# A graph message-passing layer on one core: edge factor applied in the sort, one one-hot for both sums, VectorE on pairs of units

## What is computed

```python
xn = layernorm(h) * ln_w + ln_b
w_phys = (silu(rbf @ w1 + b1) @ w2 + b2) * cutoff[:, None]      # one filter row of 256 for each edge
msg_phys = xn[col] * w_phys
q_e, k_e, v_e = Q[row], K[col], V[col]                          # 8 heads of 32
scores = sum(q_e * k_e, axis=-1) / sqrt(32) * cutoff[:, None]
attn = softmax(scores, axis=1)                                  # over the 8 heads of one edge
combined = msg_phys + gate * (attn[..., None] * v_e)
aggr = segment_sum(combined, row)
out = x + h + aggr @ wo + bo
```

## Time and profile before

| | |
|---|---|
| median of 3 runs | 5557.56 us (5555.09 to 5559.14) |
| profiled execution, its own time | 5559.19 us |
| its span, first to last instruction | 5557.3 us |
| busy: PE, PEld, DVE, ACT, POOL | 93%, 70%, 81%, 59%, 72% |
| mean granted TensorE clock | 0.972 of full |

### The profile page before, as it was taken

How to read it: one execution, slowest core, us unless ns; L and a number is a source line. 1 busy time by engine, 2 the same in 40 slices (tenths; PEclk the granted TensorE clock), 3 DMA queues, 4 the chain that set the end, 5 groups by cost and what they waited for, 6 DMA issues and landing times. The chain is left out here.

```text
span 5557.3 us, 119878 instructions
## 1 busy us (share of the span) xinstructions
PE 5156.6 (93%) x24352; PEld 3906.9 (70%) x24353; DVE 4493.7 (81%) x11381; ACT 3260.9 (59%) x11609; POOL 4001.3 (72%) x3475
## 2 busy tenths in 40 slices
PE   3879999999999999995899999999999999999999
PEld 3556666666666666674677777777777777777777
DVE  9789887666655555323899999999999999999995
ACT  4223333333333333332788888888888888888884
POOL 1567777777777777775577777777777777777770
PEclk9889999999999999997899999999999999999999
DMA  6234444444444443445999999999999999999965
GB/s 200 89 105 133 144 165 158 142 150 167 158 145 148 168 155 134 152 156 181 314 320 326 325 326 326 325 321 326 325 326 325 326 325 327 324 326 327 326 198 185
DMA packets 584358, 1305.93 MB, mean 235 GB/s; under 512 B 81230, under 2 KB 384118, under 8 KB 582945
## 3 DMA queue, kind: packets, MB, share of 16 engines
q0 software_dynamic: 221536, 881.08, 44.7%
q1 hardware_dynamic: 311780, 345.48, 20.5%
q10 hardware_dynamic: 50850, 77.03, 3.9%
HBM read 1024.15 MB, written 324.38 MB: 243 GB/s over the span
## 5 line engine op out<-in xcount | busy, mean ns | idle before, releaser
L1002 POOL DMA_INDIRECT ukvx<-kvx_table,udst x1760 | 2174.7, 1236 | 668.3 <-issue 480.9
L338 POOL DMA_INDIRECT records<-rows,slot_i x1660 | 1750.9, 1055 | 666.6 <-issue 498.2
L691 PE MATMUL w_ps<-w2s,hid 128*128 128x256 f32 x6656 | 1555.7, 388 | 47.4 <-DVE rows L605 47.3
L691 PEld LDWEIGHTS w_ps<-w2s,hid 128*128 128x128 f32 x6656 | 1251.4, 193 | 371.9 <-issue 156.9
L805 ACT ACTIVATE hid<-hid_ps,b1t 128x512 f32<-128x512 f32 x832 | 525.5, 682 | 1518.5 <-PE hid_ps L680 1504.1
L605 DVE TENSOR_TENSOR rows<-w_ps,b2b 128x512 f32<-128x512 f32 x832 | 570.9, 686 | 749.0 <-PE w_ps L691 748.9
L1118 PE MATMUL ag_ps<-ukvx,uonehot_cut 128*128 128x256 f32 x3520 | 989.3, 404 | 5.3
L1103 PE MATMUL uq_ps<-aggr,uonehotT 128*128 x3520 | 986.4, 404 | 0.0
L1122 PE MATMUL ag_ps<-ukvx,uonehot 128*128 128x256 f32 x3520 | 941.2, 392 | 41.1 <-ACT uonehot L1036 41.1
L1122 PEld LDWEIGHTS ag_ps<-ukvx,uonehot 128*128 128x128 f32 x3520 | 689.0, 196 | 139.7 <-issue 42.2
L1118 PEld LDWEIGHTS ag_ps<-ukvx,uonehot_cut 128*128 128x128 f32 x3520 | 604.8, 192 | 153.9 <-issue 6.3
(11 more groups left out here) (171 smaller groups left out, 5025.0 us busy)
## 6 DMA issues: line engine op xcount, KB each, us to landing
urec<-records SPq DMA_DIRECT2D x880, 260.0 KB
rbf_in<-in_edge_attr SPq DMA_DIRECT2D x207, 256.0 KB, 2.9
kvx_table<-kvx ACTq DMA_DIRECT2D x10, 3456.0 KB, 14.7
ukvx<-kvx_table,udst POOLq DMA_INDIRECT x1760
records<-rows,slot_i POOLq DMA_INDIRECT x1661, 2.6
records<-kvx SPq DMA_DIRECT2D x1, 13000.0 KB
fbase<-x_plus_h SPq DMA_DIRECT2D x14, 896.0 KB, 7.2
out<-fout SPq DMA_DIRECT2D x13, 896.0 KB, 4.9
```

The source lines that it names most:

```text
L338: pool.indirect_dma_start(recs, bass.IndirectOffsetOnAxis(ap=slot_i[:, q, t:t + 1], axis=0), rows[:, q, t, :], None).then_inc(scattered[q] ...
L691: m = pe.matmul(w_ps[j % 2][:, h, :], hid[:, k % 2, c, h, j * P:(j + 1) * P], w2s[:, c, :], start=(h == 0 and c == 0), stop=(c == 1), skip ...
L1002: pool.indirect_dma_start(kvx[:, k, j, :], None, table, bass.IndirectOffsetOnAxis(ap=dst_i[:, k, j:j + 1], axis=0), bounds_check=NPAD - 1, ...
```

## The change

- In the sort, ScalarE multiplies each filter row by its edge factor in place (`scale`, four tiles at a time; the first half of a group at the end of its own iteration, the second in the next), and the scatter waits for the two halves (`scaled`) instead of `w_out` and `placed`.
- In the edge stage the one-hot times factor and the one-hot times reciprocal are gone. One float32 copy of the one-hot (`widen`) serves both sums; VectorE multiplies the exponentials by the reciprocal (`normalise`) ahead of `attend`.
- `physical`, `score`, `weigh`, `maximum`, `invert`, `normalise`, `attend` and `select` each take two units with one instruction, in every second unit; `select` is one `tensor_tensor` over four halves instead of two `tensor_scalar` a unit. `exponent` handles a pair too. `query_key` stays one instruction a unit.
- `half_bucket` has bytes instead of int32. TensorE loads 32 numbers a turn, ScalarE 16, both from an offset that is a multiple of 16.

The core of the diff:

```diff
-        half_bucket = sb("half_bucket", [1, HALVES + 2 * DEPTH], I32)
+        half_bucket = sb("half_bucket", [1, HALVES + 2 * SEEN], U8)
 
         prep(nc, sem, x, src, dst, rbf, weight, w1, b1, w2, b2, ln_w, ln_b, wq, bq, wk, bk, wv, bv, wo, bo,
...
                 q = k % RING
-                pool.wait_ge(s["w_out"], g * 4 + 4)
-                pool.wait_ge(s["placed"], g + 1)
-
-                pool.sem_inc(s["placed_waited"], 1)
                 tail = isinstance(g, int) and g == LASTG
                 for t in range(LASTC if tail else GC):
+                    if t % 4 == 0:
+                        pool.wait_ge(s["scaled"], g * 2 + t // 4 + 1)
+                        pool.sem_inc(s["scaled_seen"], 1)
                     pool.indirect_dma_start(recs, bass.IndirectOffsetOnAxis(ap=slot_i[:, q, t:t + 1], axis=0),
                                             rows[:, q, t, :], None).then_inc(scattered[q], 16)
                 if tail:
+                    pool.wait_ge(s["scaled"], g * 2 + 2)
...
+            def scale(g, k, half):
+
+                q = k % RING
+                act.wait_ge(s["w_out"], g * 4 + 2 * half + 2)
+                if half == 0:
+                    act.wait_ge(s["placed"], g + 1)
+                    act.sem_inc(s["placed_seen"], 1)
+                for t in range(4 * half, 4 * half + 4):
+                    m = act.activation(rows[:, q, t, 0:H], rows[:, q, t, 0:H], ACT.Copy, scale=rows[:, q, t, R_CUT:R_CUT + 1])
...
+                        scale(g - 1, (k - 1) % BODY, 1)
                     if more:
                         silu(g + 1, k + 1, 1)
                     if more2:
                         evacuate(g + 2, k + 2)
+                    scale(g, k, 0)
                     if t is not None:
                         act.wait_ge(s["xnt_ps"], (i - 1) * NB + t + 1)
                         act.activation(xnT[:, t].rearrange("p k e -> p (k e)"), tq_ps[:, 0:H], ACT.Copy).then_inc(s["xnt_sb"], 1)
...
             act.wait_ge(s["q_stored"], 16 * BATCHES)
...
-                    sp.wait_ge(s["cut_ready"], u - (DEPTH - 1))
+                    sp.wait_ge(s["onehot_ready"], u - (DEPTH - 1))
...
+            def widen(u, k, i, first):
                 act.wait_ge(s["onehot_ready"], u + 1)
                 if not first:
                     act.wait_ge(s["ag_done"], u - (DEPTH - 1))
-                for j in range(2):
-                    m = act.activation(ohc[:, k, j, :], ohb[:, k, j, :], ACT.Copy, scale=rec[:, k, j, R_CUT:R_CUT + 1])
-                m.then_inc(s["cut_ready"], 1)
-
-            def share(u, k, i, first):
-                act.wait_ge(s["recip_done"], u + 1)
-                for j in range(2):
-                    m = act.activation(oh[:, k, j, :], ohb[:, k, j, :], ACT.Copy, scale=rc[:, k % 2, j:j + 1])
-                m.then_inc(s["share_ready"], 1)
+                act.activation(oh[:, k], ohb[:, k], ACT.Copy).then_inc(s["widened"], 1)
...
+                q = k // 2 % 2
                 act.wait_ge(s["max_done"], u + 1)
-                if not (first and k < 2):
-                    act.wait_ge(s["av_done"], u - 1)
-                for j in range(2):
-                    m = act.activation(ex[:, q, j, :], sc[:, q, j, :], ACT.Exp, bias=mx[:, q, j:j + 1], accum_out=sm[:, q, j:j + 1])
-                m.then_inc(s["exp_ready"], 1)
+                if not (first and k < 4):
+                    act.wait_ge(s["av_done"], u - 3)
+                for r in range(4):
+                    m = act.activation(ex[:, q, r, :], sc[:, q, r, :], ACT.Exp, bias=mx[:, q, r:r + 1], accum_out=sm[:, q, r:r + 1])
+                m.then_inc(s["exp_ready"], 2)
...
+                        half_bucket[0:1, 0:2 * DEPTH] if first else half_bucket[0:1, bass.ds(u * 2, 2 * DEPTH)],
...
-                exponent(u, k, i, first)
+                if k % 2:
+                    exponent(u, k, i, first)
                 if not (first and k < LAG):
-                    keep(u - LAG, bucket_of[k])
+                    keep(u - LAG, bucket_of[2 * k + 1])
...
+            _, rest = nc.values_load_multi_w_load_instructions(half_bucket[0:1, HALVES:HALVES + 2 * DEPTH], engines=[mybir.EngineType.Activation], min_val=0, max_val=BUCKETS - 1,
...
-                    pe.matmul(to[j], ohc[:, k, j, :], kvx[:, k, j, 2 * H:3 * H], start=False, stop=False, skip_group_check=True)
+                    pe.matmul(to[j], oh[:, k, j, :], kvx[:, k, j, 2 * H:3 * H], start=False, stop=False, skip_group_check=True)
                 pe.wait_ge(s["av_done"], u + 1)
-                pe.wait_ge(s["share_ready"], u + 1)
...
-                dve.wait_ge(rec_in[k], i * 16 + 16)
+                for n in range(2):
+                    dve.wait_ge(rec_in[k + n], i * 16 + 16)
                 if not first:
-                    dve.wait_ge(s["cut_ready"], u - (DEPTH - 1))
-                    dve.wait_ge(s["share_ready"], u - (DEPTH - 1))
-                    dve.wait_ge(s["turned"], u - (DEPTH - 1))
-                for j in range(2):
-                    m = dve.tensor_scalar(ohb[:, k, j, :], iota_bf[:], rec[:, k, j, R_LOC:R_LOC + 1], None, ALU.is_equal)
-                m.then_inc(s["onehot_ready"], 1)
+                    dve.wait_ge(s["widened"], u - (DEPTH - 2))
+                    dve.wait_ge(s["turned"], u - (DEPTH - 2))
+                dve.tensor_tensor(pair(ohb, k), iota_bf[:].unsqueeze(1).to_broadcast([P, 4, P]),
+                                  pair(rec, k)[:, :, R_LOC:R_LOC + 1].to_broadcast([P, 4, P]), ALU.is_equal).then_inc(s["onehot_ready"], 2)
...
+                dve.wait_ge(kvx_in[k + 1], i * 32 + 32)
+                both = pair(kvx, k)[:, :, 2 * H:3 * H]
+                dve.tensor_tensor(both, pair(rec, k)[:, :, 0:H], both, ALU.mult).then_inc(s["phys_done"], 2)
...
             def score(u, k, i, first):
...
-                    dve.wait_ge(s["exp_ready"], u - 1)
...
+                dve.tensor_reduce(sc[:, q], pair(kvx, k - 1)[:, :, 0:H].rearrange("p r (h d) -> p r h d", h=NH), AX_X, ALU.add).then_inc(s["scored"], 2)
...
-                dve.tensor_reduce(mx[:, q], sc[:, q], AX_X, ALU.max, negate=True).then_inc(s["max_done"], 1)
+                dve.tensor_reduce(mx[:, q], sc[:, q], AX_X, ALU.max, negate=True).then_inc(s["max_done"], 2)
...
+                dve.reciprocal(sm[:, q], sm[:, q]).then_inc(s["recip_done"], 2)
+
+            def normalise(u, k, i, first):
+                q = k // 2 % 2
+                dve.wait_ge(s["recip_done"], u + 1)
+                dve.tensor_tensor(ex[:, q], ex[:, q], sm[:, q].unsqueeze(2).to_broadcast([P, 4, NH]), ALU.mult).then_inc(s["shared"], 2)
...
+                dve.wait_ge(s["shared"], u + 1)
+                values = pair(kvx, k - 1)[:, :, H:2 * H].rearrange("p r (h d) -> p r h d", h=NH)
+                dve.tensor_tensor(values, values, ex[:, q].unsqueeze(3).to_broadcast([P, 4, NH, HD]), ALU.mult).then_inc(s["av_done"], 2)
...
                 query_key(u, k, i, first)
-                physical(u, k, i, first)
-                ahead(select, SELECT_AHEAD, u, k, i, first, last)
-                score(u, k, i, first)
-                behind(invert, 1, u, k, i, first)
-                weigh(u, k, i, first)
-                maximum(u, k, i, first)
-                behind(attend, 1, u, k, i, first)
+                if k % 2 == 0:
+                    physical(u, k, i, first)
+                    behind(invert, 1, u, k, i, first)
+                    behind(normalise, 1, u, k, i, first)
+                    behind(attend, 1, u, k, i, first)
+                else:
+                    score(u, k, i, first)
+                    weigh(u, k, i, first)
+                    maximum(u, k, i, first)
+                    ahead(select, SELECT_AHEAD - 1, u, k, i, first, last)
```

71 lines of the change are left out of this document (31 added, 40 removed).

## The result

The changed kernel takes 6550.82 us (median of 4 runs, 6548.81 to 6557.02), the kernel before, run beside it, 5557.38: a ratio of 1.179, 95% interval 1.1769 to 1.181. 993 us more, where the prediction had 48 less.

The account below looks back on a forecast made before the run. VectorE bounds the edge stage, TensorE nearly equal. 5559.2 - 51 (edge stage) + 4 (sort +3, last scatters -2, filling and draining +3) = 5512, less 1.6 for the median: 5510 us; 8 in 10 for 5468 to 5562.

Parts of the forecast that it names:

- Register loads: Once-a-turn loads in the edge stage, priced by 16-byte pieces: TensorE's 32 bytes 1.07 us, ScalarE's 16 bytes 0.85.
- its alternative: TensorE's register load priced by number, 64 ns each, so that it goes up by 0.32 us.
- the rival: ScalarE's load alone could double to 3.4 us with 16 numbers: 33 us, giving 5543; within a rival of chance 0.22.
- VectorE's pair: VectorE's edge-stage steps for two units: 6.19 us against 6.26 before, 3.10 a unit, dependent starts 0.04 us after their cause.
- The slack of 1.9 us: Queries done 1.9 us before VectorE wants them, covering the once-a-turn stall of 1.3; TensorE catches up 0.46 us a pair.
- TensorE becomes the bound: Rival: load by number, or stall and clock unchanged; 3.13 to 3.17 us a unit, 5518 to 5552 us; chance 0.22.
- Late records: Rival: edge-stage record loads landing after more than 6.9 us; 0.2 over gives 88 us, 5570 to 5620; chance 0.13.
- Gathers: GpSimd's two gathers a unit, 1.52 and 1.00 us, the long one containing the selects; with the new select 1.0 for both.
- the sort: ScalarE's scale passes, 0.516 us each, cost the sort 3 us; earlier scatters of the last group give -2.
- the DMA engines as no bound: Edge-stage DMA, bytes unchanged: a unit could go down to 2.71 us, so no bound at 3.12.
- passes over four rows: VectorE's passes over a pair occupy 1.13 to 1.14 us; rival that they cost two passes: 5545 to 5565, chance 0.10.
- the select at 0.61: VectorE's new select, one instruction a pair, forecast at 0.60 us against 0.66 for a pair's selects before.

Follow-up runs that it names:

- e1: The changed kernel with int32 bucket numbers again instead of bytes; 5851.92 us, 1.0522 of the kernel before.
- e5: e1 with each pair pass raising its semaphore by one instead of two; 5900.68 us, 1.0612 of the kernel before.
- e9: e5 with the select moved into the even unit, behind physical and the reciprocal; 5653.7 us, 1.0172 of the kernel before.
- e14: e5 with TensorE's register load split into 20 numbers at a turn's first unit and 12 at the fifth; 5760.97 us, 1.0373 of the kernel before.
- e7: e6 with the edge factor copied out by ScalarE, so record loads no longer wait for the pair's weights; 5572.99 us, 1.0036 of the kernel before.
- e8: The kernel before with the change's aligned loads of 32 and 16 numbers, as int32, and nothing else of it; 5539.7 us, 0.9966 of the kernel before.
- e12: e8 with TensorE's register load split into 20 and 12 numbers; 5521.17 us, 0.9933 of the kernel before.
- e13: e7 with TensorE's register load split into 20 and 12 numbers; 5410.08 us, 0.9736 of the kernel before.
- e6: e5 with the select in the even unit and attend in the odd unit; 5590.16 us, 1.0059 of the kernel before.

## Why the prediction was wrong

**Register loads: the step that failed.** The prediction read four durations as pieces of 16 bytes, 256 and 290 ns each, and so had 32 bytes at 1.07 us. Measured: 7.55. Four int32 values fill such a piece, so the same rows read "64 ns a value", which the text had as its alternative. But that alternative took the price of an int32 for a byte, +0.32 us. Both readings were fitted on int32 alone; a value of another width was outside the rows, and no row bounded it from above. The dear price stood in the earlier trace rows already, ScalarE's 1724 ns for eight, and the fit by pieces explained it away. The term that was mis-sized is 1.07 us against 7.55, 110 times; against int32 loads of the same count the bytes cost 699 us, the low clock behind them included. The Trainium skill (Runtime: NRT & Kernel Launch, Instruction fetch mechanics) has some 200 ns a register, of registers that are loaded from HBM. For bytes the runs agree within a fifth, 235 ns on TensorE and 3396/16 = 212 on ScalarE; for int32 in a row they do not, 64. The prediction quoted it with 6.4 us for this load, close to the 7.55, and then priced the rival with ScalarE's load alone, because TensorE's 87 ns seemed to refute the rule. It refuted it for int32 in a row only. By that page, 6.4 - 2.35 = 4.1 us in 110 turns would have been an estimate of 450 us more, and that belonged in the range. Without the bytes the forecast would have failed as well: e1's 5852 us lie 290 above the range, by the next two steps.

**VectorE's pair: right in its passes, wrong in its gaps.** Forecast 6.19, measured 6.68. Of the 0.49 us between them, 0.30 are five dependent starts that came 0.10 instead of 0.04 us after their cause, 0.12 the step from maximum to select (0.23 where 0.11 stood), and only 0.07 the passes themselves. With increments of one (e5) the pair is 6.3, so most of the difference is the waits that stand as instructions of their own. The prediction took the gap from the old code, where each rise was one, and did not see that the diff changes the increments. It had (6.26 - 6.19) x 440 = 31 us won by the pairs; (6.7 - 6.26) x 440 = 194 us were lost, in e1 as in the changed kernel. Even the 6.3 of e5 is not below the 6.26 of before: in the order of the change, pairs save VectorE nothing.

**The slack of 1.9 us did not exist.** The prediction let TensorE catch up 0.46 us a pair and so cover the pause. But the turn of a pair's first unit needs the select, now the last step of the pair: TensorE waits for it (159.9 us, 173 times), and what it would gain in pace it can't store ahead of the load. e9 and e14 show both sides of this, 1.4 and 1.3 us a turn of the 3.6 left over in e5. The stall makes up the rest of e1's 290 us, about 100.

**"TensorE becomes the bound": right in kind, too small.** The rival had 3.13 to 3.17 us a unit by a pause of 1.3 and 0.8 us of clock. e7, with VectorE at 2.94, ran at 3.22. The pause is 1.3 by PE's own row; by the row of PEld it was 174.4/102 = 1.7 before, and 197.0/100 = 2.0 in e7. e8 shows that already the kernel before paid for over half of it. That VectorE and TensorE were nearly equal bounds, 25.0 and 25.1 us a turn, fits the runs with int32 loads of the same count: beside e8, the change with its quickest pairs is 33 us slower (e7), the split load alone 19 us faster (e12), and both together are 130 us faster (e13). Why e7 is slower than e8, with less work on VectorE and the same load, stays open.

**Late records: the mechanism is there, its price depends on the rest.** In the changed kernel the median landing is 5.5 us, inside the 6.9 allowed, though ScalarE waits for records 121 times from 2750 to 5300 us, 139.1 us in all; what that costs there no run shows. In e6 and e9 the wait is longer, and freeing the buffer early is worth 17 us in the one and 76 in the other, close to the rival's 88.

**Gathers: the wrong culprit.** The prediction blamed the selects for 1.52 against 1.00. In the changed kernel, from 3998.87 on, with attend from 3998.87 to 4000.10 and the select from 4002.64 to 4003.33:

```profile
3998.44 1.01 POOL L1018 DMA_INDIRECT ukvx<-kvx_table,udst  x1 [0.30 <-issue]
3999.75 1.22 POOL L1018 DMA_INDIRECT ukvx<-kvx_table,udst  x1 [0.30 <-issue]
4001.28 1.01 POOL L1018 DMA_INDIRECT ukvx<-kvx_table,udst  x1 [0.30 <-issue]
4002.59 1.01 POOL L1018 DMA_INDIRECT ukvx<-kvx_table,udst  x1 [0.30 <-issue]
```

Only the one that starts while attend is running is long: 0.35 us of attend were left, and 0.35 + 0.88 = 1.23. Of the 521 gathers from 2700 us on that start while attend or physical alone is running, 519 last what is left of the pass plus 879 ns, within 15 ns; the 320 that start under the score, which has one input, last 1.00 to 1.02 us. In the earlier trace rows the long gather starts at 3992.52, 0.04 after physical, and 0.64 + 0.88 = 1.52: physical, not the select inside it. Nor is the new select harmless, as the prediction had it. In the changed kernel hardly a gather starts under it (4), but in e5 317 do, and 316 of them are long by the same sum, as this one:

```profile
4007.91 0.69 DVE L1181 TENSOR_TENSOR uonehot_bf<-uiota_bf,urec 128x512 bf16<-128x512 bf16 x1
4008.11 1.37 POOL L1021 DMA_INDIRECT ukvx<-kvx_table,udst  x1 [0.30 <-issue]
```

The Trainium skill (SBUF — State Buffer, Who interferes with whom) says that a VectorE instruction with two inputs in SBUF contends with a GpSimd instruction that reads SBUF. These rows agree, if the gather counts as one (its `udst` lies in SBUF), and the prediction had used only what the passage says of `tensor_scalar`. No run shows a time that hangs on it; in the changed kernel GpSimd was not the bound.

**Right:** the sort (+1 us forecast, 1.0005 measured; the scale passes take 505 ns against 516 forecast), the DMA engines as no bound down to 3.04 us a unit (333 GB/s), passes over four rows at 1.13 us, and the select at 0.61.

## What to carry over

Where one engine's instruction stream pauses once a turn, ask what is queued on it just then: a step that was moved to the end of its pair emptied the queue, and a pause that had been covered in part cost its full length and the low clock behind it. Two bounds that are equal must be relieved together; each alone gives little. A price read from rows of one width, count or increment holds for that one: when the diff changes any of them, the range has to reach as far as the dearest rule at hand.

## What was not expected of the hardware

- A register load of bytes costs 234 to 235 ns a value on TensorE and 212 on ScalarE, of int32 in a row 64 on both. ScalarE's every second one of 16 int32 costs 215 each, as bytes do. 32, 20, 16 and 12 int32 took TensorE 2134, 1372, 1112 and 848 ns; 27 and 7 took 2348 and 1066, about 0.5 us more than such a line gives. Whether the count or the offset makes these 0.5 us, no run tells apart.
- In these kernels a pass that raises a semaphore by two does not carry the wait for its own inputs: the wait is an instruction ahead of it, and the dependent start is 0.10 us after its cause instead of some 0.04 (e1 and e5).
- The granted clock went to 1.2 GHz after TensorE had stood still for 7.8 us (the changed kernel), for 2.5 (e5) and for 1.7 (e14, 82 times in 2550 us). With waits of 1.6 us it fell less often in e12 (15 times), and with waits of 0.6 us in e13 once.
- A gather that starts while a VectorE `tensor_tensor` with both inputs in SBUF is running (physical, attend or the new select) lasts until 0.88 us after that pass; one that starts first keeps its 1.00 us.
